# Leaving out 17 waits of a mixer step and aligning TensorE's loop in a megakernel of a recurrent mixer and experts

## The chip, the cores and the metric

The program runs on one NeuronCore of a Trainium2 chip. The metric is device time of one execution in microseconds, the median over several executions. Matmuls run on TensorE (PE), whose weight loads are shown apart (PEld); the other engines are VectorE (DVE), ScalarE (ACT), GpSimd (POOL) and SyncE (SP), which issues most DMAs. Each engine reads its own list of instructions, and engines meet only through semaphores. The granted clock of TensorE is shown as a share of full speed; it has two levels, 2.4 GHz and half of it.

## The reference

x has shape (2, 4096, 512), float32. It is normalised row by row, and the result goes two ways, whose outputs are added to x.

```
xn = layernorm(x)
x + mixer(xn) + experts(xn)
```

The mixer is a recurrence over 4096 time steps with 16 heads of 32 channels. Per head it keeps a 32x32 state:

```
sab = S @ kk
S   = S * exp(w) + outer(sab, b) + outer(v, k)
y   = S @ r
```

Here r, w, k, v, kk and b come from projections of a mix of each row with the one before it, through small two-stage (low-rank) projections, tanh and sigmoid. y is normalised per head, gets a bonus term and a gate, and is projected by `output`. The experts route the 8192 rows to 8 experts with 1024 rows each by a balanced assignment, and each runs a 512-2048-512 network with gelu.

## The kernel before

The mixer (`time_mix`) cuts time into tiles of 64 steps for both sequences, 128 rows in all. There are 64 tiles. Inside a tile the recurrence is solved in two chunks of 32 steps with matrices of 32x32: the inverse of a triangular matrix is built by doubling, in the five stages `inverse_stage(k)` for k = 1, 2, 4, 8 and 16 (line 1028, 64 small matmuls each), and scores between queries and keys are made by `score("u", m)` and `score("y", m)` for m = 0 to 5 (line 1043).

The work is a software pipeline with five parts: N (norm of the rows), A (projections), B (scores), C (inverse, state), D (normalise, gate, output). One call of `step` issues one part of each for five different tiles. `step` is called for five steps of filling, then in a hardware loop (`nc.Fori`) whose body has LONG = 28 steps written out and which runs twice, then for seven steps at the end. Behind the mixer come the experts, with the routing between their matmuls.

The order on each engine is the order of the calls in `on_tensor`, `on_vector` and so on; nothing reorders it. In a step TensorE goes, among other things, through the stages k = 1, 2, 4, 8, 16 of the inverse, `low("low_k", 2)` (line 1004) between k=8 and k=16, `key_of` (line 995), `low_second` (line 1189) and the scores, one after another.

With its 45 wait instructions a step has 3345 instructions on TensorE: 1650 weight loads and 1650 matmuls beside them.

Of the kernel before, what the change touches and what calls it, by code (L numbers as in the profile page):

```python
# [9 lines left out]
B, T, C = 2, 4096, 512  # L10
# [7 lines left out]
ROW = C + 4  # L18
SETS = 4
LONG = 28  # L20

class Steps:
# [96 lines left out]
def time_mix(nc, core, dram):  # L120

    pe, dve, act, pool = core.pe, core.dve, core.act, core.pool
    with ExitStack() as ctx:
# [862 lines left out]
        def on_tensor(e, turn, on, out, got):  # L987
            at = COLUMNS[turn % 2]
            Ns, A, Bs, Cs, D = (n in on for n in "NABCD")
# [18 lines left out]
            def inverse_stage(k, half):  # L1008

                if half == 0:  # L1010
                    clear(e, f"S{k}")
                    clear(e, f"S{k}+")
                    if k == 1:
                        if "C.rows1" in dve.was:
                            e.wait_ge(dve.old, dve.ago("C.rows1"))
                        e.wait_ge(pool.old, pool.ago("B.e1"))
                    else:
                        e.wait_ge(act.sem, act[f"C.S{k // 2}"])
                        e.wait_ge(pool.sem, pool[f"C.b{k // 2}"])
                taken = {1: slice(0, N), 16: slice(N, 2 * N)}.get(k, slice(0, 2 * N))  # L1020
                by = raw_of(0) if k == 1 else grow
                for i in range(half * HALF_U // 2, (half + 1) * HALF_U // 2):
                    for n in (i, i + HALF_U):
                        turned_in = TURN * (n // HALF_U) * (k in (4, 16))
                        turned_out = TURN * (n // HALF_U) * (k in (2, 8))
                        for h in range(HG):
                            rows, to = head((h + turned_in) % HG), head((h + turned_out) % HG)
                            mm = e.matmul(both_banks[to, n * 2 * N + taken.start:n * 2 * N + taken.stop], by[rows, blk(n)],  # L1028
                                          got["ew"][rows, n * 2 * N + taken.start:n * 2 * N + taken.stop],
                                          start=True, stop=True, skip_group_check=True)  # L1030
                if half:
                    mm.then_inc(pe.sem, pe.step(f"C.S{k}"))

            def score(q, *which):

                for m in which:
                    clear(e, f"{q}{m}")
                    e.wait_ge(dve.sem, dve["B.kk0"])
                    e.wait_ge(pool.sem, pool[f"B.q{q}"])
                    n0, n1 = UNITS[m]  # L1040
                    for n in range(n0, n1):
                        for h in range(HG):
                            mm = e.matmul(BANK[f"{q}{m}"][head(h), (n - n0) * 2 * KEYS:(n - n0 + 1) * 2 * KEYS],  # L1043
                                          queries[q][head(h), blk(n)], keys[head(h), n * 2 * KEYS:(n + 1) * 2 * KEYS],
                                          start=True, stop=True, skip_group_check=True)
                    mm.then_inc(pe.sem, pe.step(f"B.{q}{m}"))
# [134 lines left out]
                mm.then_inc(pe.sem, pe.step("A.decay"))  # L1181

            def low_second():
                for name in ("mk", "aaa", "ma"):
                    clear(e, name)
                e.wait_ge(act.sem, act["A.k"])
                for g in range(G):
                    for i, name in enumerate(("key", "mk", "aaa", "ma")):
                        mm = e.matmul(BANK[name][:, g * P:(g + 1) * P], wt["low_w2"][head(i), g * P:(g + 1) * P], hid4[head(i), :],
# [139 lines left out]
        step(-1, 3, "NABC")  # L1329
        step(0, 4, "NABCD")  # L1330
        turns = (tiles - 8) // LONG
        with nc.Fori(0, turns) as part_of_tiles:
            for i in range(LONG):
                step(part_of_tiles * LONG + (i + 1), SETS + 1 + i, "NABCD")
# [575 lines left out]
```

## Time and profile before

| | us |
|---|---|
| median of 3 runs | 5907.34 |
| lowest, highest | 5901.49, 5909.01 |
| the profiled execution | 5900.49 |
| its span, first to last instruction | 5898.6 |
| TensorE busy | 5437.2 (92%) |
| VectorE busy | 3741.3 (63%) |
| ScalarE busy | 2014.6 (34%) |

The mean granted clock is 0.972. The mixer fills the span up to about 3950 us, its loop runs from 232.6 to 3619.8 us; the experts fill the rest. Busy shares add up instructions, and small matmuls on different quarters of the array overlap, so busy TensorE is not TensorE at its peak. Idle time in front of a group of instructions is put down to what ended it. "issue" means that nothing in the profile ended it.

### The profile page before, as it was taken

Reading aid. Unit: us, or ns where it says so; the run is one execution under the profiler, and the core shown is the slowest. Engines: PE = TensorE matmul, PEld = TensorE weight load, DVE = VectorE, ACT = ScalarE, POOL = GpSimd, SP = SyncE. Lnnn points to the kernel's source line nnn. Section 1 sums busy time; section 2 is a strip of 40 time slices with the busy share of each in tenths; the row PEclk is TensorE's granted clock in tenths of the full one; section 3 lists DMA queues with packets and bytes.
Section 4 is the critical chain, followed back from the end, with each engine's and each line's share of the span. In section 5 each row is a group of like instructions: output and inputs, shape, how many; then the busy total and the mean of one; then the engine's idle time right before and its main releaser. Section 6 shows DMA issues by size and latency. Waiting matters only on the chain. (4 is left out here: it accounts for less than half of the span.)

```text
span 5898.6 us, 243936 instructions
## 1 busy us (share of the span) xinstructions
PE 5437.2 (92%) x110664; PEld 3805.1 (65%) x110664; DVE 3741.3 (63%) x9004; ACT 2014.6 (34%) x3659; POOL 1396.8 (24%) x1156
## 2 busy tenths in 40 slices
PE   6999999999989999899999999975999999999998
PEld 6777777777777777777777777752444444444443
DVE  6788888788888788878888888845232232232310
ACT  4444444444444444444444444420000000000000
POOL 1222222222222222222222222212022022121220
PEclk9999999999999999999999999987999999999999
DMA  1001000010100000010000000003112112112110
GB/s 62 23 18 25 18 21 22 18 25 18 25 18 23 21 20 24 18 25 18 23 20 23 21 20 23 16 16 97 61 50 93 50 52 102 50 52 99 39 64 14
DMA packets 108638, 211.07 MB, mean 36 GB/s; under 512 B 25553, under 2 KB 26705, under 8 KB 107089
## 3 DMA queue, kind: packets, MB, share of 16 engines
q1 hardware_dynamic: 92240, 144.91, 8.4%
q0 software_dynamic: 15360, 50.48, 2.6%
q8 instruction: 878, 14.39, 1.0%
q14 instruction: 160, 1.30, 0.1%
HBM read 144.60 MB, written 50.72 MB: 33 GB/s over the span
## 5 line engine op out<-in xcount | busy, mean ns | idle before, releaser
L392 DVE COPY_PREDICATED time_raw<-time_known,w_bank 128x96 f32<-128x96 int32 (+6 forms) x3072 | 816.7, 274 | 214.0 <-PE w_bank L1043 128.5
L1862 PE MATMUL moe_bank<-moe_w,moe_hidden 128*128 128x512 f32 x2048 | 930.4, 597 | 0.0
L1849 PE MATMUL moe_bank<-moe_hT,moe_w 128*128 128x512 f32 x2048 | 924.3, 594 | 1.5 <-DVE moe_hT L1743 1.5
L1764 ACT ACTIVATE moe_hidden<-moe_bank,moe_b 128x512 f32<-128x512 f32 x256 | 175.9, 687 | 1635.3 <-PE moe_bank L1849 1635.3
L1849 PEld LDWEIGHTS moe_bank<-moe_hT,moe_w 128*128 128x128 f32 x2048 | 386.5, 190 | 471.7 <-issue 469.8
L1862 PEld LDWEIGHTS moe_bank<-moe_w,moe_hidden 128*128 128x128 f32 x2048 | 379.8, 190 | 429.7 <-issue 428.2
L909 POOL TENSOR_TENSOR time_grow<-time_eye,time_grow 128x512 f32<-128x512 f32 x256 | 371.7, 1452 | 1131.6 <-DVE time_grow L418 1131.6
L1028 PE MATMUL w_bank<-time_ew,time_grow 32*32 32x64 f32 x32768 | 403.8, 218 | 160.4 <-issue 143.6
L1028 PEld LDWEIGHTS w_bank<-time_ew,time_grow 32*32 32x32 f32 x32768 | 350.7, 104 | 199.4 <-issue 157.2
L1043 PE MATMUL w_bank<-time_keys,time_queries_u 32*32 32x160 f32 x8192 | 362.5, 309 | 31.5 <-issue 20.3
L1743 DVE COPY moe_hT<-moe_bank 128x512 f32<-128x512 f32 x64 | 44.2, 691 | 501.0 <-PE moe_bank L1834 501.0
L661 ACT COPY time_ew<-w_bank 128x1024 f32<-128x1024 f32 x192 | 193.9, 1010 | 467.4 <-DVE time_grow L418 467.1
L1043 PE MATMUL w_bank<-time_keys,time_queries_y 32*32 32x160 f32 x8192 | 330.9, 297 | 17.4 <-DVE time_mixed L507 15.6
L1043 PEld LDWEIGHTS w_bank<-time_keys,time_queries_y 32*32 32x32 f32 x8192 | 234.5, 105 | 111.2 <-DVE time_k L527 35.6
L1043 PEld LDWEIGHTS w_bank<-time_keys,time_queries_u 32*32 32x32 f32 x8192 | 241.3, 109 | 97.3 <-issue 30.9
L995 PE MATMUL w_bank<-time_xf,time_key_w 128*128 128x128 f32 x2048 | 284.6, 296 | 11.8 <-issue 11.8
L405 DVE SCALAR_TENSOR_TENSOR time_lerp<-w_bank,time_maa,time_xx 128x128 f32<-128x128 f32 x1024 | 283.7, 339 | 13.9 <-PE w_bank L1097 12.0
L995 PEld LDWEIGHTS w_bank<-time_xf,time_key_w 128*128 128x128 f32 x2048 | 264.9, 209 | 31.1 <-issue 31.0
L995 PE MATMUL w_bank<-time_xf,time_receptance 128*128 128x128 f32 x2048 | 282.7, 287 | 0.3 <-issue 0.3
L1802 POOL DMA_INDIRECT out<-moe_result,moe_slots x64 | 69.3, 1083 | 876.1 <-DVE moe_result L1753 861.8
L995 PEld LDWEIGHTS w_bank<-time_xf,time_value 128*128 128x128 f32 x2048 | 255.7, 196 | 31.6 <-issue 31.3
L418 DVE STREAM_TRANSPOSE time_grow<-w_bank 128x512 f32<-128x512 f32 x256 | 182.7, 714 | 139.8 <-PE w_bank L1028 139.6
(226 smaller groups left out, 9421.5 us busy)
## 6 DMA issues: line engine op xcount, KB each, us to landing
moe_w<-in_w SPq DMA_DIRECT2D x64, 1024.0 KB, 7.4
mid_xn<-time_xn_rows SPq DMA_DIRECT2D x128, 129.0 KB, 2.5
time_x_rows<-in_x SPq DMA_DIRECT2D x128, 128.0 KB, 2.7
time_base<-in_x SPq DMA_DIRECT2D x128, 128.0 KB, 3.0
mid_acc<-time_mixed SPq DMA_DIRECT2D x128, 128.0 KB, 2.4
mid_scores<-time_rated SPq DMA_DIRECT2D x128, 2.0 KB, 1.7
moe_b<-in_b SPq DMA_DIRECT2D x8, 256.0 KB, 12.8
time_key_w<-in_w_key_w SPq DMA_DIRECT2D x1, 1024.0 KB, 5.3
```

The lines of the kernel that those rows point to most:

```text
L392: e.copy_predicated(by_raw[:, "uy".index(q), n0:n1, :, 0:8 * j + 8], known[:, "uy".index(q), :, :, mine].to_broadcast([P, n1 - n0, 2, 8 * ...
L405: e.scalar_tensor_tensor(grp(lerp, g), grp(BANK[f"delta{f}"], g), wt["maa"][:, f * G + g:f * G + g + 1], grp(xx, g), ALU.add, ALU.mult).th ...
L418: e.transpose(chunks(grow), rest_of(both_banks)).then_inc(dve.sem, dve.step(f"C.t{k}"))
L661: e.copy(col(got["ew"]), inv_bank).then_inc(act.sem, act.step(f"C.S{k}"))
L909: e.tensor_tensor(chunks(grow), every_unit(wt["eye2"]), chunks(grow), ALU.subtract).then_inc(pool.sem, pool.step(f"C.b{k}"))
L995: mm = e.matmul(ps[:, o * P:(o + 1) * P], weight[:, g * width + o * P:g * width + (o + 1) * P], rhs_of(g), start=g == 0 and (o == 0 or not ...
L1028: mm = e.matmul(both_banks[to, n * 2 * N + taken.start:n * 2 * N + taken.stop], by[rows, blk(n)], got["ew"][rows, n * 2 * N + taken.start: ...
L1043: mm = e.matmul(BANK[f"{q}{m}"][head(h), (n - n0) * 2 * KEYS:(n - n0 + 1) * 2 * KEYS], queries[q][head(h), blk(n)], keys[head(h), n * 2 * ...
L1764: e.activation(hidden[now % 4][:, :], up[now % 3][:, :], ACT.Gelu_apprx_tanh, bias=b1[:, x * FC + k:x * FC + k + 1]).then_inc(act.sem, act ...
L1802: e.indirect_dma_start(dram["out"], slot(x, t), tile(result, t), None).then_inc(core.stored, 16)
L1849: got = e.matmul(up[now % 3][:, :], w1[:, g * F + k * P:g * F + (k + 1) * P], hT[x % 2][:, g * CAP + half * HALF:g * CAP + (half + 1) * HA ...
L1862: got = e.matmul(down[t][:, :], hidden[now % 4][:, t * P:(t + 1) * P], tile(w2, k), start=k == 0, stop=k == FC - 1)
```

## The change

The order on every engine stays. Three places lose waits on TensorE:

- `inverse_stage` no longer waits for the former readers of its two banks, except at k=1, and not for C.rows1 of the step before;
- `score` waits for the keys (B.kk0) and the queries (B.qu, B.qy) only in its first unit, m = 0;
- `low_second` has one wait, on A.tail, for its four.

That makes 28 wait instructions in a step for 45, and 3328 instructions for 3345. Lines behind line 18 move by one or two in the new file.
```diff
+PAGE = 256
@@ inverse_stage
                 if half == 0:
-                    clear(e, f"S{k}")
-                    clear(e, f"S{k}+")
                     if k == 1:
-                        if "C.rows1" in dve.was:
-                            e.wait_ge(dve.old, dve.ago("C.rows1"))
+                        clear(e, "S1")
+                        clear(e, "S1+")
                         e.wait_ge(pool.old, pool.ago("B.e1"))
                     else:
                         e.wait_ge(act.sem, act[f"C.S{k // 2}"])
@@ score
                     clear(e, f"{q}{m}")
-                    e.wait_ge(dve.sem, dve["B.kk0"])
-                    e.wait_ge(pool.sem, pool[f"B.q{q}"])
+                    if m == 0:
+                        e.wait_ge(dve.sem, dve["B.kk0"])
+                        e.wait_ge(pool.sem, pool[f"B.q{q}"])
@@ low_second
-                for name in ("mk", "aaa", "ma"):
-                    clear(e, name)
-                e.wait_ge(act.sem, act["A.k"])
+                e.wait_ge(act.sem, act["A.tail"])
@@ time_mix
         turns = (tiles - 8) // LONG
+        nc.tensor.addr_align(PAGE, offset=154)
         with nc.Fori(0, turns) as part_of_tiles:
```

On TensorE, from the second score unit to the third in a step of the loop, the kernel before has this. In brackets stand the engines whose semaphores the instruction, and the wait instructions ahead of it, wait for; w_bank is PSUM, time_ew and time_grow the two factors of the inverse, time_xf the mixed rows.

```order
L1043 MATMUL w_bank<-time_keys,time_queries_u 32x160 [waits pool_steps0,dve_steps0]
L1043 MATMUL w_bank<-time_keys,time_queries_u 32x160 x11
L1028 MATMUL w_bank<-time_ew,time_grow 32x64 [waits act_steps0,pool_steps0]
L1028 MATMUL w_bank<-time_ew,time_grow 32x64 x63
L1004 MATMUL w_bank<-time_xf,time_low_k 128x128 [waits dve_steps0]
L1004 MATMUL w_bank<-time_xf,time_low_k 128x128 x3
L995 MATMUL w_bank<-time_xf,time_key_w 128x128 [waits act_steps0]
L995 MATMUL w_bank<-time_xf,time_key_w 128x128 x7
L1028 MATMUL w_bank<-time_ew,time_grow 32x32 [waits act_steps0,pool_steps0]
L1028 MATMUL w_bank<-time_ew,time_grow 32x32 x63
L1043 MATMUL w_bank<-time_keys,time_queries_u 32x160 [waits pool_steps0,dve_steps0]
L1043 MATMUL w_bank<-time_keys,time_queries_u 32x160 x11
```

The same stretch of TensorE after the change:

```order
L1043 MATMUL w_bank<-time_keys,time_queries_u 32x160 [waits dve_steps0]
L1043 MATMUL w_bank<-time_keys,time_queries_u 32x160 x11
L1027 MATMUL w_bank<-time_ew,time_grow 32x64 [waits pool_steps0,act_steps0]
L1027 MATMUL w_bank<-time_ew,time_grow 32x64 x63
L1005 MATMUL w_bank<-time_xf,time_low_k 128x128 [waits dve_steps0]
L1005 MATMUL w_bank<-time_xf,time_low_k 128x128 x3
L996 MATMUL w_bank<-time_xf,time_key_w 128x128 [waits act_steps0]
L996 MATMUL w_bank<-time_xf,time_key_w 128x128 x7
L1027 MATMUL w_bank<-time_ew,time_grow 32x32 [waits pool_steps0,act_steps0]
L1027 MATMUL w_bank<-time_ew,time_grow 32x32 x63
L1043 MATMUL w_bank<-time_keys,time_queries_u 32x160 [waits dve_steps0]
L1043 MATMUL w_bank<-time_keys,time_queries_u 32x160 x11
```

No matmul has moved. The score units have lost POOL's semaphore; the two stages of the inverse have one wait instruction in front of them for two, and still wait for ACT and POOL.

## Rows read from the trace of the kernel before

**Rows 1.** The page, parts 1 and 3: busy us; queue, packets, MB, share of 16 engines.
```profile
PE 5437.2 (92%) x110664; PEld 3805.1 (65%) x110664; DVE 3741.3 (63%) x9004; ACT 2014.6 (34%) x3659; POOL 1396.8 (24%) x1156
...
q8 instruction: 878, 14.39, 1.0%
```
**Rows 2.** Waits of PE: who waited for whom: us in total, times, longest us.
```profile
PE w_bank L1028 <- issue: 158.6, 110, 2.8
...
PE w_bank L1189 <- ACT time_tail L755: 15.3, 62, 1.4
```
**Rows 3.** Timeline of PE, stage k=2, loop steps one and two: start, us, group, idle before.
```profile
242.93 1.07 PE L1028 MATMUL w_bank<-time_ew,time_grow 32*32 32x64 f32 x85
245.89 0.68 PE L1028 MATMUL w_bank<-time_ew,time_grow 32*32 32x64 f32 x43 [1.89 <-issue]
...
304.07 1.00 PE L1028 MATMUL w_bank<-time_ew,time_grow 32*32 32x64 f32 x76
```
**Rows 4.** DMA from 254.8 to 256.0 us (packets, MB, share); timeline of low_k.
```profile
q8 instruction: 1, 0.02, 5.9%
...
257.28 1.37 PE L1004 MATMUL w_bank<-time_xf,time_low_k 128*128 128x128 f32 x8 [2.04 <-DVE time_grow L418]
```
**Rows 5.** Windows, the loop body's two turns: us; busy of each engine; clock; DMA.
```profile
232.60:1927.40 1694.80, 1558.86 (x46200) 1282.96 (x46200) 1400.51 (x3503) 797.88 (x1486) 453.24 (x366) 0.98 0.09 21
1927.40:3619.80 1692.40, 1561.09 (x46201) 1285.27 (x46201) 1394.33 (x3498) 796.25 (x1482) 447.66 (x362) 0.98 0.09 21
```
**Rows 6.** Windows of single steps: us; PE, PEld, DVE, ACT, POOL busy; clock; DMA.
```profile
232.60:293.70 61.10, 56.32 (x1650) 46.57 (x1650) 49.76 (x125) 28.65 (x53) 16.22 (x13) 0.97 0.09 21
1142.50:1204.50 62.00, 57.20 (x1651) 47.90 (x1651) 49.86 (x126) 28.64 (x53) 16.25 (x13) 0.94 0.08 21
2836.50:2897.20 60.70, 55.96 (x1651) 46.48 (x1651) 49.78 (x126) 28.65 (x53) 16.24 (x13) 0.97 0.09 21
3741.10:3801.20 60.10, 54.77 (x1650) 44.95 (x1650) 49.89 (x125) 28.59 (x53) 16.25 (x13) 1.00 0.07 17
1441.80:1499.60 57.80, 54.63 (x1651) 44.96 (x1651) 49.95 (x126) 28.33 (x53) 16.23 (x13) 1.00 0.09 22
957.20:1019.60 62.40, 55.87 (x1650) 45.82 (x1650) 49.82 (x126) 28.54 (x53) 16.25 (x13) 0.97 0.08 21
```
**Rows 7.** Timeline of PE in the steps from 2836.5, 3741.1 and 3679.4 us.
```profile
2849.57 0.67 PE L1028 MATMUL w_bank<-time_ew,time_grow 32*32 32x64 f32 x43 [1.63 <-issue]
...
2861.26 1.05 PE L1004 MATMUL w_bank<-time_xf,time_low_k 128*128 128x128 f32 x8 [2.34 <-DVE time_raw L392]
2862.15 3.34 PE L995 MATMUL w_bank<-time_xf,time_key_w 128*128 128x128 f32 x16
...
3765.28 1.16 PE L1004 MATMUL w_bank<-time_xf,time_low_k 128*128 128x128 f32 x8 [1.79 <-DVE time_raw L392]
3766.28 1.95 PE L995 MATMUL w_bank<-time_xf,time_key_w 128*128 128x128 f32 x16
...
3770.35 0.33 PE L1028 MATMUL w_bank<-time_ew,time_grow 32*32 32x32 f32 x25 [1.12 <-issue]
...
3708.83 0.33 PE L1028 MATMUL w_bank<-time_ew,time_grow 32*32 32x32 f32 x17 [1.49 <-issue]
```
**Rows 8.** Timeline of PE in the step from 1441.8 us: its groups with over 0.2 us of idle time.
```profile
1445.81 0.32 PE L1028 MATMUL w_bank<-time_ew,time_raw 32*32 32x32 f32 x13 [0.51 <-issue]
...
1460.79 1.43 PE L1043 MATMUL w_bank<-time_keys,time_queries_u 32*32 32x160 f32 x36 [0.33 <-issue]
...
1464.66 0.66 PE L1028 MATMUL w_bank<-time_ew,time_grow 32*32 32x64 f32 x42 [1.43 <-issue]
...
1475.83 1.17 PE L1189 MATMUL w_bank<-time_hid,time_low_w 32*128 32x128 f32 x32 [0.23 <-ACT time_tail L755]
...
1490.26 0.75 PE L1043 MATMUL w_bank<-time_keys,time_queries_y 32*32 32x160 f32 x16 [0.29 <-DVE time_mixed L507]
```
**Rows 9.** Timeline of PE at the start of the loop body's second turn.
```profile
1927.44 1.09 PE L1122 MATMUL w_bank<-time_ident,time_xn_rows 128*128 128x128 f32 x4 [3.97 <-PEq L341]
```

## The prediction

> **What bounds the kernel now.** I read the shares first: TensorE (PE) is busy 5437.2 of 5898.6 us [rows 1], so the question is what its idle time is made of. The waits view then shows that in the mixer this is mostly no wait for data. 158.6 us stand before the 32x32 matmuls of line 1028 with the releaser "issue", 110 times, which means that nothing in the profile held them back; the longest regular wait on another engine, for ACT at line 1189, takes 15.3 us over 62 steps [rows 2].
>
> The timeline shows where those stops sit. In the loop's first step (from 232.6 us) TensorE runs 85 matmuls of the stage at line 1028, stands still for 1.89 us and runs the other 43. In the next step the same stage is cut after 76 [rows 3]: 9 matmuls earlier, each with its own weight load, so about 18 instructions. A step has 1650 matmuls, 1650 weight loads [rows 6] and 45 wait instructions, together 3345, and 3345 is 13 times 256 and 17 over. A grid of 256 instructions laid over TensorE's program would slide by 17 a step, as the stops do. The DMA view names the grid: queue 8 moved 878 packets of kind "instruction", 14.39 MB, 16.4 KB each [rows 1], which is 256 instructions of 64 bytes, and one of them ran in the 1.2 us in the middle of the 2.04 us stop before line 1004 [rows 4]. So a page of 256 instructions is fetched as the sequencer comes to its end, and TensorE stops if what is queued before the boundary lasts less than the fetch. Counting from the stops, every page of the kernel before starts at the same place, and the loop's first instruction stands at slot 153 of its page.
>
> I then laid the boundaries over the step. Most of the 13 cost nothing, because slow 128x128 matmuls are queued or the stage starts with a wait during which the sequencer runs ahead. They cost where the 256-instruction stages of line 1028 are half consumed. The step from 1441.8 us has three stops, 0.51, 0.33 and 1.43 us [rows 8], and takes 57.8 us; the step from 957.2 us, with its boundaries half a page further, takes 62.4 [rows 6].
>
> **The change part by part.** 17 waits go, so a step has 3328 instructions, exactly 13 pages, and every step of the loop has the boundaries at the same places. The alignment stands ahead of the loop's register move: the move gets slot 154, the loop's first wait 155, and the first boundary comes 101 instructions into each step, then every 256. I placed the 13 in the new order: ten fall where the steps before lose nothing or under 0.2 us. Three matter.
>
> First, 613 instructions in: 170 slots into the stage k=2 of line 1028, after 85 matmuls. That is the place of the first loop step: 1.89 us in one step and 1.63 in another [rows 3, 7]. I take 1.8.
>
> Second, 1381 in: one matmul into the four of low_k (line 1004). In the loop's first step the boundary stands one matmul earlier, at the head of low_k, and costs 2.04 us [rows 4]; the others read are 2.34 and 1.79 [rows 7]. One more 128-wide matmul of cover is worth 0.1 (16 of them take 1.95 us [rows 7]), so 1.9.
>
> Third, 1637 in: 105 matmuls into stage k=16. After 103 it cost nothing in the step from 2836.5 us and 1.12 us in the step from 3741.1; after 111 it cost 1.49 [rows 7]. The difference between the first two is the clock: the second stop let the granted clock fall (0.97 over the step from 2836.5, 1.00 over the one from 3741.1 [rows 6]), the 16 matmuls of line 995 then took 3.34 us and not 1.95 [rows 7], and that longer stretch covered the fetch. So each step pays one of two: 1.4 us of lower clock, or 1.1 us of a third stop. Four of the five steps that have this place paid the clock. I take 1.4, and 0.3 for a second stretch at the lower clock in one step out of four or five (0.94 over the step from 1142.5 [rows 6]).
>
> The base is the step from 1441.8: 57.8 less 0.51, 0.33 and 1.43 is 55.5 [rows 6, 8]. New step: 55.5 + 1.8 + 1.9 + 1.4 + 0.3 = 60.9. As a control, the four steps before with their boundaries there took 61.1, 62.0, 60.7 and 60.1, mean 61.0 [rows 6]. The step before is, on average over its phases, (1694.8 + 1692.4)/56 = 60.5 with the two ends of the loop body in it [rows 5]; TensorE stands 3.97 us at such an end [rows 9], I take 5 us with what follows, so 60.3 without. Both kernels have the two ends. The difference is +0.5 to +0.7; with 0.1 off for the later place of the second boundary, +0.55 a step. The 56 loop steps and the four full steps behind them (two instructions further, same places) make 60: +33 us.
>
> The removed waits themselves. They are passed already when they are reached, as far as their engines tell: later waits of the same engine cover them. What they cost is bounded by idle time. In the step from 1441.8 TensorE is idle 57.8 - 54.63 = 3.17 us, of which 2.27 are the three stops and 0.23 + 0.29 are waits on ACT and DVE that the change keeps [rows 6, 8]. 0.38 us is left for all the rest. So removing 17 gives between nothing and 0.38 us a step; at the very most 0.9, if the idle time before lines 1189 and 1043 (a reader of two of the removed and one) went with them. I take 0.05, nearer to nothing, since almost all idle time of that step has another name: -3 us.
>
> The alignment pads once, before the loop, with idle instructions: from nothing to 255 of them. No row shows one; the trace's cheapest bounds are 0 and the spacing of a small matmul in its stage, 1.07 us for 85 [rows 3], 13 ns each, 3 us for 255. I take 0 to 1. Steps ahead of the loop and the experts behind it keep their work; their pages shift, but the waits view names no "issue" before the experts' matmuls of 512 columns.
>
> Sum: 5900.5 (the profiled execution; its span is 5898.6) + 33 - 3 = 5930. The median of the runs shown is 5907.3, the range 5901.5 to 5909.0, so the profiled execution lies 7 us under it, and part of that may come on top. I keep 5930, +0.4% on the median.
>
> The Trainium skill, "Runtime: NRT & Kernel Launch", section "Instruction fetch mechanics", says that the sequencer fetches the next 256-instruction page while it executes the current one, and that a crossing is "mostly hidden". By that rule all phases cost alike and the change would be worth only its waits, 5907 or a little less. The trace agrees on the page of 256 and on ten of the 13 crossings, and not on the others: the stops of 1.4 to 2.3 us move with the grid [rows 3, 7]. This is the second rival below, reckoned from rows.
>
> **The rivals.**
> The third stop and the lower clock both. For it: a stop of 1.49 us stands only 6 matmuls on [rows 7], and the waits that go change how far the sequencer is ahead. Against it: in the four steps at a lower clock line 995 covered the fetch. It adds 1.1 us in four of five steps, +53: 5983. It decides if the fetch at instruction 1637 starts more than 0.5 us later than now.
> The places don't matter as much as I read: the stops and the stretches of lower clock average out, the removed waits give back 0.2 to 0.4 us a step, and nothing moves beyond 0.2%: 5907. For it: four control steps are few, with a spread of 1.9 us.
> Faster: the wait instructions are on the path. Some stand before the very instructions that show idle time, lines 1189 and 1043, and a sequencer that has 17 fewer to handle is further ahead at each boundary. If it gives the full 0.9 us a step, -54, and the second stop shrinks by a third, -0.6 a step, -36, the sum is 5900 + 33 - 90 = 5843. It decides once the waits return over 0.6 us a step. Against it: the step from 1441.8 has no more than 0.38 us of idle time that isn't named after a page or another engine [rows 6, 8].
> The alignment doesn't land there. If it were without effect, the loop would begin 49 slots earlier, at 106, with the first boundary after 150: the steps like it took 62.4 us or more [rows 6], +2.1 a step, 6026. If it counts from another origin, any phase is possible, down to 57.8, -2.5 a step: 5750.
>
> **How the numbers follow.** Forecast 0.45, third stop with lower clock 0.10, no change 0.22, faster by the waits 0.15, misplaced 0.08, half of it to each side. A difference under 0.2%, 12 us, can't be told from none. The forecast itself spreads by the clock (0.3 us a step either way, 18 us) and lies above 5919 in about 8 of 10. Slower: 0.37 + 0.10 + 0.04 + 0.04 = 0.55; same 0.25; faster 0.20. The forecast's own range is 5912 to 5950. The range of 8 in 10 takes in no change, half of the fast rival and most of the third stop: 5880 to 5970.
>
> **What would show it.** In the profile after: every loop step's stage k=2 splits 85 and 43 with 1.6 to 1.9 us of "issue" between; low_k splits 1 and 7 with 1.7 to 2.3 us; stage k=16 splits at 105 in steps at full clock, and only there; no stop in stages k=1, 4 and 8 inside the loop, where now they wander. "issue" on line 1028 is then some 110 us, with more before low_k. Steps differ by the clock alone, near 60.8 us. It would be wrong if the splits stand elsewhere (misplaced), if the two stops are under 1.3 us (the waits held the sequencer back), or if a step without any stop is shorter than 55.5 us (the waits were on the path).

## The result, and the profile after

| | median us | lowest to highest | runs | ratio to before (95%) |
|---|---|---|---|---|
| before | 5905.6 | 5901.5 to 5909.9 | 6 | |
| after | 5933.8 | 5924.0 to 5941.0 | 6 | 1.0047 (1.0034 to 1.0059) |

The changed kernel is slower by 0.47%, 28 us. Its profiled execution is the slowest of its six (5941.0 us, span 5939.2), so the difference of the two traces, 40.6 us, is larger than that of the medians.

The page of the kernel after, parts 1 and 3: TensorE's work has not grown, and a few fewer pages of instructions are fetched [rows 1].

```profile
PE 5428.0 (91%) x110664; PEld 3811.6 (64%) x110664; DVE 3733.7 (63%) x9004; ACT 2023.2 (34%) x3659; POOL 1405.7 (24%) x1156
...
q8 instruction: 874, 14.32, 1.0%
```

Its waits of TensorE (total us, times, longest). Against [rows 2] "issue" before the stages of short matmuls (now line 1027) has grown from 158.6 to 182.7 us, and a second entry, 98.3 us at low_k (line 1005), was not among the large ones before. The wait for ACT has shrunk from 15.3 to 12.8 us.

```profile
PE w_bank L1027 <- issue: 182.7, 114, 2.4
PE w_bank L1005 <- issue: 98.3, 56, 2.1
...
PE w_bank L1187 <- ACT time_tail L756: 12.8, 64, 1.4
```

The timeline of the loop step that starts at 425.6 us, its groups around the stops (start, us, group, idle time before). These answer to [rows 3, 4, 7].

```profile
435.94 1.06 PE L1027 MATMUL w_bank<-time_ew,time_grow 32*32 32x64 f32 x85
439.08 0.67 PE L1027 MATMUL w_bank<-time_ew,time_grow 32*32 32x64 f32 x43 [2.08 <-issue]
...
448.36 0.38 PE L1005 MATMUL w_bank<-time_xf,time_low_k 128*128 128x128 f32 x1
450.42 0.94 PE L1005 MATMUL w_bank<-time_xf,time_low_k 128*128 128x128 f32 x7 [1.69 <-issue]
451.20 1.95 PE L996 MATMUL w_bank<-time_xf,time_key_w 128*128 128x128 f32 x16
453.08 1.09 PE L1027 MATMUL w_bank<-time_ew,time_grow 32*32 32x32 f32 x105
455.31 0.30 PE L1027 MATMUL w_bank<-time_ew,time_grow 32*32 32x32 f32 x20 [1.15 <-issue]
```

The stage k=2 is cut after 85 of 128 matmuls, low_k after 1 of 8, the stage k=16 after 105. All 56 loop steps have the first two cuts, and 42 of 56 the third; k=1, k=4 and k=8 are never cut inside the loop. Idle time, as I counted it over the timeline of all 56: k=2 mean 1.75 us (1.51 to 2.08), low_k mean 1.76 (1.34 to 2.10), k=16 mean 1.34 where it occurs (0.84 to 2.08).

Each of these stops goes with a fetched page. The DMA view from 447.8 to 449.0 us, around the start of the stop at low_k (448.73 to 450.42 us), has one packet:

```profile
q8 instruction: 1, 0.02, 5.8%
```

It starts at 447.9 us, 0.8 us before TensorE stops, and TensorE goes on 1.4 us after it has ended. So it is with all 154 stops of the loop, read from the trace's packet times: the last packet of queue 8 starts 0.1 to 1.7 us before TensorE stops, and TensorE goes on 1.2 to 1.6 us after that packet's end.

The next step back, from 363.4 us, shows the other course. The clock row under it is a windows row of 390.90 to 394.10 us (us; busy of PE, PEld, DVE, ACT, POOL; granted clock; DMA).

```profile
390.06 1.05 PE L1005 MATMUL w_bank<-time_xf,time_low_k 128*128 128x128 f32 x7 [2.07 <-issue]
390.90 3.51 PE L996 MATMUL w_bank<-time_xf,time_key_w 128*128 128x128 f32 x16
```
```profile
390.90:394.10 3.20, 3.20 (x16) 3.20 (x16) 2.83 (x7) 0.63 (x2) 1.29 (x2) 0.50 0.02 5
```

Directly after the second stop the granted clock is 0.50, the lower level of 1.2 GHz. The 16 matmuls of line 996 take 3.51 us and not 1.95, and stage k=16 is not cut. In the step from 970.5 us the stretch of lower clock begins earlier, 14.1 us into the step and behind the first stop; line 996 then runs at full clock and k=16 is cut:

```profile
997.41 1.95 PE L996 MATMUL w_bank<-time_xf,time_key_w 128*128 128x128 f32 x16
...
1002.13 0.30 PE L1027 MATMUL w_bank<-time_ew,time_grow 32*32 32x32 f32 x20 [1.75 <-issue]
```

Single steps and whole parts, after (same columns), to be read against [rows 5, 6]:

```profile
425.60:485.60 60.00, 54.31 (x1651) 44.71 (x1651) 49.76 (x126) 28.58 (x53) 16.24 (x13) 1.00 0.09 21
363.40:425.60 62.20, 57.32 (x1650) 47.75 (x1650) 49.78 (x126) 28.67 (x53) 16.24 (x13) 0.95 0.08 21
970.50:1032.40 61.90, 55.92 (x1650) 46.31 (x1650) 49.83 (x126) 28.56 (x53) 16.25 (x13) 0.97 0.09 21
...
237.90:3650.20 3412.30, 3113.18 (x92401) 2572.78 (x92401) 2785.56 (x6998) 1601.82 (x2966) 906.11 (x726) 0.98 0.09 21
3650.20:3834.80 184.60, 167.11 (x4950) 138.75 (x4950) 149.41 (x376) 85.76 (x159) 48.74 (x39) 0.97 0.08 19
```

The same two stretches of before:

```profile
232.60:3619.80 3387.20, 3119.94 (x92401) 2568.23 (x92401) 2794.84 (x7001) 1594.13 (x2968) 900.89 (x728) 0.98 0.09 21
3619.80:3801.20 181.40, 165.52 (x4950) 136.06 (x4950) 149.50 (x375) 85.67 (x159) 48.71 (x39) 0.99 0.08 20
```

So of the 40.6 us between the two spans, 5.3 lie ahead of the loop (237.9 less 232.6), 25.1 in it (60.93 us a step in place of 60.49), 3.2 in the three full steps behind it and 7.0 in what follows (2104.4 in place of 2097.4). The loop's two totals have chance in them: the one step that passes from the body's first turn to its second took 68.5 us before and 63.0 after, by its stretches of lower clock. The 54 steps that are neither the first nor this one last 60.33 us before and 60.85 after. Of the first, 3.65 us are one gap at the loop's entry, which before did not have:

```profile
237.92 1.09 PE L1122 MATMUL w_bank<-time_ident,time_xn_rows 128*128 128x128 f32 x4 [3.65 <-SPq L307]
```

### The profile page after: what moved, and what is told of

Same layout as the page of the kernel before. It is cut to its first block and busy times, and to the rows that moved or that the text cites. A ratio compares the mean times of both kernels' runs of the same rounds, so it can differ in the third digit from the quotient of the medians.

```text
span 5939.2 us, 242899 instructions
## 1 busy us (share of the span) xinstructions
PE 5428.0 (91%) x110664; PEld 3811.6 (64%) x110664; DVE 3733.7 (63%) x9004; ACT 2023.2 (34%) x3659; POOL 1405.7 (24%) x1156
## 5 line engine op out<-in xcount | busy, mean ns | idle before, releaser
L1043 PE MATMUL w_bank<-time_keys,time_queries_u 32*32 32x160 f32 x8192 | 349.4, 302 | 9.7 <-issue 2.2
L946 POOL TENSOR_TENSOR time_ew<-time_eye,time_ew 128x512 f32<-128x512 f32 x64 | 87.9, 1374 | 756.6 <-DVE time_ew L490 756.6
## 6 DMA issues: line engine op xcount, KB each, us to landing
moe_b<-in_b SPq DMA_DIRECT2D x8, 256.0 KB
```

Source lines behind the costliest of these rows:

```text
L946: e.tensor_tensor(rest_of(out["ew"]), every_unit(wt["eye2"]), sum_of(out["ew"]), ALU.subtract).then_inc(pool.sem, pool.step("B.e1"))
```

## The experiments

The theory, A: a step's time is set by which matmuls stand at the page boundaries, and the alignment put them at a poor place. The rivals: the removed waits matter by themselves; aligning costs by itself; the clock falls for other reasons. "Slot" is the slot of 256 at which the loop's first instruction stands; the step column is the loop's time in one traced execution over 56, with both ends of the body in it. Two executions with the same stops can differ in it by 0.7 us, as after and "155, padding at start" do, so it is no measure of small differences.

| run | slot | median us | ratio to before (95%) | us a step |
|---|---|---|---|---|
| before | 153, slides by 17 | | | 60.49 |
| after | 155 | 5933.8 | 1.0047 (1.0034 to 1.0059) | 60.93 |
| waits only | 106 | 6084.3 | 1.0290 (1.0264 to 1.0316) | 63.37 |
| slot 238 | 238 | 5752.5 | 0.9725 (0.9701 to 0.9749) | 57.85 |
| waits as filler | 155, slides | 5983.1 | 1.0110 (1.0090 to 1.0131) | 61.58 |
| alignment only | 155, slides | 5922.5 | 1.0004 (0.9991 to 1.0018) | 60.64 |
| slot 196 | 196 | 5842.7 | 0.9869 (0.9853 to 0.9886) | 59.37 |
| slot 0 | 0 | 5757.7 | 0.9730 (0.9716 to 0.9744) | 57.78 |
| 238, padding at start | 238 | 5736.2 | 0.9697 (0.9682 to 0.9712) | 57.88 |
| waits spread | 155, slides | 5927.1 | 1.0025 (1.0011 to 1.0038) | 60.83 |
| 248, padding at start | 248 | 5729.2 | 0.9697 (0.9678 to 0.9717) | 57.89 |
| 155, padding at start | 155 | 5914.7 | 1.0018 (1.0005 to 1.0032) | 60.25 |
| stop inside k=16 | 155, slides | 6011.7 | 1.0178 (1.0158 to 1.0198) | 62.37 |

Each ratio is to runs of before on the same chip, and for small differences it is the ratio that counts; their medians there were 5915.9, 5916.8 and 5905.0 us for the three groups of runs in the order of the table.

### The waits alone

```
-        nc.tensor.addr_align(PAGE, offset=154)
```

> The 17 waits are left out as in the changed kernel, the alignment is not made, so the loop's first instruction lies at slot 106 and each of its steps still crosses the same 13 places. Theory A (the time is set by which matmuls lie at the crossings): the crossings move by 49 instructions, to after 150 instructions of a step and every 256 from there; steps of before with their first crossing there lasted 62.4 to 63.0 us, so about 62.9 a step, +2.6 x 60 over before's 60.3: about 6060 us, 6020 to 6075. Theory B (the changed kernel is slower through its alignment's padding or through the lost waits, the places do not matter): with the padding gone 5900 to 5935 us.

Measured 6084.3 us, 9 above the range of A; B is out. The steps run from 61.5 to 65.1 us, and the one over the body's end takes 69.0. One of them, from 551.2 us, and its cuts at the new places:

```profile
551.20:616.00 64.80, 59.20 (x1651) 48.74 (x1651) 49.86 (x126) 28.55 (x53) 16.22 (x13) 0.92 0.08 20
```
```profile
564.53 0.41 PE L1027 MATMUL w_bank<-time_ew,time_grow 32*32 32x64 f32 x19 [1.67 <-issue]
570.75 0.69 PE L1027 MATMUL w_bank<-time_ew,time_grow 32*32 32x64 f32 x44 [0.31 <-issue]
...
583.12 1.82 PE L1043 MATMUL w_bank<-time_keys,time_queries_u 32*32 32x160 f32 x23 [2.11 <-issue]
584.87 3.78 PE L996 MATMUL w_bank<-time_xf,time_key_w 128*128 128x128 f32 x16
```

Leaving the waits out is therefore the half of the change that fixes the boundaries' places, and without the alignment it fixes them at a place that costs 2.9 us a step more than before. The alignment of the changed kernel takes back 2.4 of these.

### Slot 238

```
-        nc.tensor.addr_align(PAGE, offset=154)
+        nc.tensor.addr_align(PAGE, offset=237)
```

> The changed kernel with the loop's first instruction at slot 238 of 256 in place of 155. Theory A (places): the crossings come after 18 instructions of a step and every 256 from there; steps of before with a first crossing near there lasted 58.2 to 58.5 us, so about 2 us a step less than before's 60.3 and 2.5 less than the changed kernel's 60.9: 5906 + 4 (entry) - 1.9 x 60 = about 5795 us, 5770 to 5820. Theory B (alignment or lost waits cost, the places do not): 5930 to 5950 us, more by the longer padding (132 in place of 49).

Measured 5752.5 us, below A's range and far from B. The stops of the step from 365.3 us, all of its groups with idle time before them:

```profile
369.44 0.32 PE L1027 MATMUL w_bank<-time_ew,time_raw 32*32 32x32 f32 x13 [0.61 <-issue]
380.03 1.16 PE L1172 MATMUL w_bank<-time_rk,time_bonus_ones 128*128 128x128 f32 x8 [0.16 <-DVE time_mixed L454]
384.46 1.42 PE L1043 MATMUL w_bank<-time_keys,time_queries_u 32*32 32x160 f32 x36 [0.25 <-issue]
387.99 0.64 PE L1027 MATMUL w_bank<-time_ew,time_grow 32*32 32x64 f32 x40 [1.09 <-issue]
398.97 1.17 PE L1187 MATMUL w_bank<-time_hid,time_low_w 32*128 32x128 f32 x32 [0.18 <-ACT time_tail L756]
413.39 0.75 PE L1043 MATMUL w_bank<-time_keys,time_queries_y 32*32 32x160 f32 x16 [0.28 <-DVE time_mixed L508]
```
```profile
365.30:422.70 57.40, 54.60 (x1650) 44.88 (x1650) 50.09 (x126) 28.34 (x53) 15.71 (x13) 1.00 0.09 22
```

The step is the twin of before's step from 1441.8 us [rows 6, 8], stop for stop. The whole loop has only 8 stretches at 0.50, against 38 before and 44 after. The clock is a part of what made the forecast too high: before's four steps with a boundary at this place (from 533.9, 1441.8, 2228.3 and 3136.1 us) took 58.2, 57.8, 59.3 and 57.6 us, mean 58.2, and one of these four has such a stretch, where the loop at slot 238 has one in seven steps. Shorter stops, 2.0 us a step and not 2.2, are as large a part, and the rest is that I took 58.4.

The gap at the loop's entry is larger here:

```profile
246.27 1.09 PE L1122 MATMUL w_bank<-time_ident,time_xn_rows 128*128 128x128 f32 x4 [9.64 <-PEq L342]
```

### The 17 waits back, in one row

```
             on_tensor(nc.tensor, turn, on, out, got)
+            if on == "NABCD":
+                for _ in range(35):
+                    nc.tensor.wait_ge(act.sem, act["A.tail"])
```

(The compiler puts two waits into one instruction and lets a last one ride on the next matmul: 35 make 17 instructions.)

> The changed kernel with 17 instructions put back at the end of each full step, as waits on a semaphore that has been reached since long: a step has 3345 instructions again and its crossings slide by 17 from step to step as in before, but the 17 waits are gone from the stages where they stood. Theory A (the waits cost nothing where they stood, the sliding places give the mean): as before plus the entry's padding, 5905 + 4 = about 5909 us, 5900 to 5918, steps 60.2 to 60.4. Rival (the removed waits cost 0.38 to 0.9 us a step on TensorE and the alignment takes it back and more): 5850 to 5885 us.

Neither: 5983.1 us. The filler was no neutral filler. From the trace, the step from 420.08 us and the one behind it:

```profile
420.08 0.63 PE L1122 MATMUL w_bank<-time_ident,time_xn_rows 128*128 128x128 f32 x4 [1.70 <-PEq L342]
...
478.14 0.63 PE L1122 MATMUL w_bank<-time_ident,time_xn_rows 128*128 128x128 f32 x4 [1.79 <-PEq L342]
```

17 waits that are all reached stop TensorE for 1.7 us or more when they stand in a row, which is at least 0.1 us each; how much more the queue hides there, the trace doesn't show. The run says nothing on what the removed waits had cost where they stood, since the new stop also gives the fetches and the other engines time. It had to be made again with the waits apart.

### The alignment alone

```
 (before, with all its waits)
+        nc.tensor.addr_align(256, offset=154)
```

> The kernel before with the alignment alone; its steps keep 3345 instructions, so the loop's first lies at slot 155 in the first turn only and the crossings go on sliding. Theory A: no difference but the padding's own price at the loop's entry, at most the 3.7 us seen there in the changed kernel: 5906 to 5912 us. Rival (the alignment itself is what costs, through its padding or what stands behind the loop): 5925 to 5940 us.

Measured a ratio of 1.0004 (0.9991 to 1.0018), 5922.5 beside 5915.9 us: no difference; its loop took 60.64 us a step beside 60.49. The directive moves the loop by two slots here and pads almost nothing. In a loop whose step is no multiple of 256 it has nothing to hold.

### Slots 196 and 0

```
-        nc.tensor.addr_align(PAGE, offset=154)
+        nc.tensor.addr_align(PAGE, offset=195)      (and offset=255)
```

> The changed kernel with the loop's first instruction at slot 196; the crossings come after 60 instructions of a step and every 256 from there: 316, 572, 828, 1084, 1340 and 1596 lie near or in the stages of short matmuls. Theory A (the places set the time): steps of before with a first crossing near 60 lasted 59.2 to 59.4 us, between those of slot 238 (58.4 by the same rows) and of slot 155 (60.7); the run of slot 238 gave 57.7, so 58.6 to 59.4 a step here: 5830 us, 5795 to 5860, with 90 slots of padding at the entry (6.6 us). Theory C (any place other than those of slot 155 is equally good, since only the matmuls at 613 and 1381 matter): 5752 less the shorter padding, 5745 to 5755.

> The changed kernel with the loop's first instruction at slot 0: crossings at 0, 256, 512, 768, 1024, 1280 and 1536. By the durations of before's sliding steps (57.96 against 58.4 us at 18) it should be 0.4 us a step faster than slot 238: 5730 us. By the stops of single crossings (1024: 1.1 us and 1280: 0.8 to 1.1 in the run with the sliding steps, against 0.3 at 1042 and 1.2 at 1298 at slot 238) it should be 0.4 a step slower: 5780 us. Theory A holds in either case; it tells which of the two rows is to be used for a forecast.

5842.7 and 5757.7 us. At slot 196 the steps are cut after 64 of k=2 and after 109 of k=8, as the step from 481 us shows, and take 59.4 us:

```profile
493.77 0.84 PE L1027 MATMUL w_bank<-time_ew,time_grow 32*32 32x64 f32 x64 [1.27 <-issue]
504.31 0.41 PE L1027 MATMUL w_bank<-time_ew,time_grow 32*32 32x64 f32 x19 [1.19 <-issue]
```

Theory C is out: places other than 155 are not equally good. Slot 0 came out between its two estimates, 57.78 against 57.85 us a step at slot 238, with somewhat longer stops and fewer stretches of lower clock (4 in the loop). Both kernels paid for their padding at the entry:

```profile
242.56 1.09 PE L1122 MATMUL w_bank<-time_ident,time_xn_rows 128*128 128x128 f32 x4 [6.60 <-PEq L342]
```
```profile
246.72 1.08 PE L1122 MATMUL w_bank<-time_ident,time_xn_rows 128*128 128x128 f32 x4 [10.97 <-PEq L342]
```

3.65, 6.60, 9.64 and 10.97 us for 49, 90, 132 and 150 slots: 73 to 75 ns a slot each time. With no padding, in the run with the waits alone, there is no such gap.

### The padding moved to the program's start

```
+        nc.tensor.addr_align(PAGE, offset=197)
         nc.tensor.wait_ge(core.consts_in, CONSTS)
 ...
-        nc.tensor.addr_align(PAGE, offset=154)
```

> Slot 238 as in the fastest run so far, with the 132 slots of padding moved from the loop's entry to the program's first instructions, where TensorE waits 16.3 us for the constants; the steps of the start and of the end get the same places. If the padding costs some 73 ns a slot on TensorE wherever it is executed in front of work: 9.6 us less at the entry, nothing at the start, and 3 to 8 us less in the two full or nearly full steps before the loop: 5752 - 10 - 5 = 5737 us, 5730 to 5745. If the gap at the entry is not the padding but the loop's own entry: 5745 to 5755.

Measured 5736.2 us. The loop starts at 225.3 and not at 246.2 us: 9.6 us of padding and 11 us in the steps ahead of the loop, where 3 to 8 were expected and whose boundaries have moved too. The first matmul waits for the constants as before, the padding lies inside that wait:

```profile
16.55 1.84 PE L255 MATMUL w_bank<-time_cent,time_lerp 128*128 128x8 f32 x8 [16.55 <-DVE time_gcent L247]
```

### The 17 waits back, one by one

```
+            def spare():
+                if on == "NABCD":
+                    e.wait_ge(act.sem, act["A.tail"])
+                    e.wait_ge(act.sem, act["A.tail"])
 ...
             if A:
                 low_second()
+            spare()                (and behind 16 more stages)
```

> As the run with 17 waits in one row at the end of a step (steps of 61.5 us, each with a new stop of 1.7 us at its first matmul), but the 17 are spread one by one over the last third of the step, behind 17 different stages. Crossings slide again by 17 a step. If a single wait that is long reached is hidden by the queue and only many in a row run it dry: the stop at the step's first matmul goes and steps last 61.5 - 1.7 = 59.8 (should the 17 removed waits have cost some 0.5 us a step where they stood) or 60.3 (should they have cost nothing): 5880 or 5910 us. If each wait costs its 0.1 us wherever it stands: steps 61.4, 5975 us.

Measured 5927.1 us, ratio 1.0025 (1.0011 to 1.0038). The stop at the step's first matmul is gone: what costs there is the row. But some single waits showed; this step from 534.2 us has new idle times at lines 1114 and 1056:

```profile
576.72 1.95 PE L1114 MATMUL w_bank<-time_output,time_mixed 128*128 128x512 f32 x4 [0.19 <-DVE time_raw L393]
...
582.47 0.75 PE L1043 MATMUL w_bank<-time_keys,time_queries_y 32*32 32x160 f32 x16 [0.18 <-DVE time_mixed L508]
583.52 1.52 PE L1056 MATMUL w_bank<-time_by_values,time_vT 32*32 32x96 f32 x64 [0.30 <-ACT time_yT L672]
```

Over all 56 steps line 1114 waits 34 times, 6.8 us in all, and line 1056 56 times, 15.3 us, while the usual wait at line 1043 has fallen from before's 14.3 us to 10.3. That is 0.32 us a step that the filler itself costs: 60.83 - 0.32 = 60.51, beside before's 60.49. So close an agreement is partly luck, since single executions differ by more. By the medians (10.3 us over before, of which 2.3 are this kernel's gap at the loop's entry and 18 the filler) the removed waits come out at some 10 us, about 0.2 us a step. So where they stood, the 17 waits cost nothing that shows clearly, and hardly more than 0.2 us a step.

### The best place, and the changed kernel's own with its padding at the start

```
-        nc.tensor.addr_align(PAGE, offset=197)
+        nc.tensor.addr_align(PAGE, offset=207)      (and offset=114)
```

> Padding at the program's start as in the fastest run, the loop's first instruction at slot 248: crossings after 8 instructions of a step and every 256 from there (264, 1032, 1288). At 0 the steps lasted 57.70 us and at 18 57.67 to 57.75. If the time changes smoothly with the place: 57.5 to 57.9 a step, 5736 us, 5722 to 5748. If two crossings that lie just behind a stage's start (1032 in the first score stage, 264 in the first inverse stage) trade against each other sharply: more than 0.5 us a step off, above 5765 or below 5706 us.

> The changed kernel's own slot (155), with its 49 slots of padding at the program's start. If the changed kernel is slower by the places of the crossings: its steps stay at 60.9 us, only the entry's 3.6 us and some 2 to 5 us in the two steps before the loop go: 5934 - 4 - 3 = 5927 us, 5920 to 5932, still above the kernel before. If a good part of its loss lies in aligning inside the program: 5905 us or less.

Slot 248 gave 5729.2 us: on the plateau from 238 over 248 to 0, not to be told apart from slot 238, and with it the fastest kernel of the study, 3% below before.

Slot 155 with the padding at the start gave 5914.7 us, 12 runs from 5892 to 5939, ratio 1.0018 (1.0005 to 1.0032). That is under my range by 5 us and above the 5905 of the other case, and the loss that is left is at the bound of what can be told from none. Its trace is of its fastest run: stops as in the changed kernel (98.8 us at low_k, 57 times), 26 stretches of lower clock in the loop in place of 44, 60.25 us a step. Ahead of the loop 8.1 us went (3.65 of padding, the rest steps with better places). Between this run and the changed kernel's profile, the loop differs by 38 us with the stops at the same places; 6 us are shorter stops (247 us in all in place of 253), and the rest goes with the 18 fewer stretches of lower clock. That much of a single run of this kernel is chance. The medians are another matter: the ratio fell by 0.29%, 17 us, of which 8 lie ahead of the loop. Where the other 9 went is open.

### A stop put among the short matmuls

```
                 inverse_stage(16, 0)
+                if on == "NABCD":
+                    for _ in range(35):
+                        e.wait_ge(act.sem, act["C.S8"])
                 inverse_stage(16, 1)
```

> As the run with 17 filler instructions in one row at the end of each step (a stop of 1.7 us in front of the step's first matmul, steps of 61.5 us, 34 windows of the lower clock in the loop), but the row stands in the middle of the stage k=16, among the short matmuls, behind a semaphore that this stage has waited for already. Theory C1 (the clock falls after a stop among the short matmuls, not after one at the step's first): far more than 34 windows, 55 to 110, each some 1.4 to 2.1 us: steps of 62.0 to 63.5 us, 6015 to 6100 us. Theory C2 (where the stop stands does not matter to the clock): 30 to 40 windows, steps near 61.5, 5970 to 5995 us.

Measured 6011.7 us, by the ratios 0.7% or 40 us more than with the same row at the step's end, and 59 stretches of lower clock in the loop where that run had 34. 31 of them begin 30 to 35 us into a step, directly behind the new stop; there that run had 10. C1 holds, at the low end of the count that it gave and 3 us under its time. One place of each kind was tried, so it isn't shown if it is the short matmuls around the stop that matter or something else of the place.

The two kernels' first loop steps are alike up to low_k, and so the pair shows one more thing. With the row at the step's end:

```profile
252.40 0.67 PE L1027 MATMUL w_bank<-time_ew,time_grow 32*32 32x64 f32 x43 [1.51 <-issue]
263.69 0.94 PE L1005 MATMUL w_bank<-time_xf,time_low_k 128*128 128x128 f32 x7 [1.63 <-issue]
268.59 0.30 PE L1027 MATMUL w_bank<-time_ew,time_grow 32*32 32x32 f32 x20 [1.16 <-issue]
```

With the row inside k=16:

```profile
253.44 0.67 PE L1027 MATMUL w_bank<-time_ew,time_grow 32*32 32x64 f32 x43 [1.51 <-issue]
...
264.73 0.94 PE L1005 MATMUL w_bank<-time_xf,time_low_k 128*128 128x128 f32 x7 [1.63 <-issue]
267.38 0.75 PE L1027 MATMUL w_bank<-time_ew,time_grow 32*32 32x32 f32 x64
269.74 0.71 PE L1027 MATMUL w_bank<-time_ew,time_grow 32*32 32x32 f32 x62 [1.60 <-issue]
```

The second half of k=16 runs through. The row moves the boundary from 105 to 96 matmuls into the stage, but there is no cut there either. What differs is the pause 32 matmuls ahead of it, which gave the fetch its time; that this is the cause is argued from the pair and not tried alone. A stretch of lower clock ahead of the boundary did the same in the changed kernel's step from 363.4 us.

## Why the prediction was right

**The places.** The three stops stand where the count put them, at 85, 1 and 105 matmuls, the first two in every loop step, the third in 42 of 56, and no page stop stands elsewhere. This was the core of the argument, and five fixed slots confirm it: by sliding steps of before with the same boundaries I expected 62.9, 58.4, 59.3, 60.9 and 58.0 us for slots 106, 238, 196, 155 and 0, and the loops gave 63.4, 57.9, 59.4, 60.9 and 57.8. The order is right in all of them and the size within 0.6 us. One proof of the fetch was misread: the packet shown in [rows 4] runs from 254.8 us on, and the stop from 255.24 to 257.28 us, so it lies at the stop's start and not in its middle. As in the changed kernel, TensorE goes on 1.4 us after the packet's end; the stop is longer than what is left of the fetch.

**The two stops.** 1.8 and 1.9 were taken, 1.75 and 1.76 measured. That one matmul further into low_k saves anything isn't shown: in the three full steps behind the loop the boundary stands at the head of low_k again, and the stop is 1.85, 1.51 and 1.94 us, mean 1.77.

**The third place: right sum, wrong mechanism in part.** "Pays one of two" was too tidy. Over the 59 full steps from the loop's first on I counted 20 steps with the third stop at full clock, 8 without it and one stretch of lower clock, 6 without it and two stretches, and 25 with both. What decides is where the stretch lies. All 14 steps of the loop without the third stop have a stretch of lower clock that begins between 24.6 and 27.5 us into the step, around the second stop and over line 996, and no other step of the loop has one there. The same holds without exception for the 9 such steps of the run with slot 155 and the padding at the start. So "pays one of two" is right for a stretch at that place. What the forecast missed is that stretches begin elsewhere too, and that many steps have none.

In its outcome, though not by its condition (a later fetch), the rival of both together is true in more than four steps of ten. It did not bring its +53 us, since the stretches of lower clock come less often than in the four steps read: 20 steps have none. Clock and third stop together cost a step about 60.9 less 55.1 less 3.5, 2.3 us, where I had 1.7. That is also why "issue" on the short matmuls is 182.7 us and not the 110 I named: the third stop was no exception. 23 of the 44 stretches in the loop begin 10 to 15 us into a step, about the first stop.

**The base.** 55.5 came from one step of before. The clean step from 425.6 us leaves 60.0 - 2.08 - 1.69 - 1.15 = 55.1; at slot 238 the step from 365.3 us leaves 57.4 - 0.61 - 0.25 - 1.09 = 55.45, the old base again. I had named a step under 55.5 us without its stops as a sign that the waits were on the path, and 55.1 is under it. At slot 238, where the same waits are gone, the sign doesn't come, so at most the place and the waits together could bring it. Of the 0.4 between the two kernels 0.3 is busy time of TensorE (54.60 against 54.31), and 0.16 is the idle time before line 1172 that only the second of the two has. Steps of before at the changed kernel's places give no clear answer. The step from 3741.1 us, at full clock, leaves 55.6 without its stops, beside 55.1; the one from 2836.5, with one stretch of lower clock, 56.7 beside 56.3 to 56.8; the one from 1142.5, with two, 58.0 beside 58.1 (the changed kernel's steps with as many stretches and no third stop). What these tenths are stays open.

The mean of 60.9 came out right because 0.4 too much here and 0.2 too much for the two stops stand against 0.6 too little for the third place. That they cancel is luck.

**The removed waits.** -3 us is not contradicted, but not measured either. At slot 238 the sum that gave 0.38 us of unexplained idle time gives 57.4 - 54.60 - 1.95 - 0.18 - 0.28 = 0.39, so this time is still there and was not that of the waits; without its stops the step is 0.1 us shorter than its twin (55.45 against 55.55). The spread filler puts the waits between nothing and 0.2 us a step. The rival with the waits on the path, 5843 us, is out by the run with the waits alone. What it assumed does exist, a wait instruction takes some time of the sequencer, but it showed only in a row and, one by one, at two places of 17.

**The alignment.** Its padding is the term that was mis-sized: 0 to 1 us taken, 3 us given as the most for 255 slots, 3.65 us measured for 49. The nearest row, the spacing of a small matmul, was the wrong neighbour by a factor of almost six.

**Ahead of the loop and behind it.** I took these to stay; they did not quite. 1.6 us ahead beside the padding, and 7.0 us in what follows the full steps, were added in the traces. The part behind the full steps took 2104.4 and 2104.7 us in the two kernels of slot 155, 2093.6 and 2093.4 in the two of slot 238, and 2107.2 in the run with the waits alone, so it, too, goes by the place; which of its stages pays was not tried. The forecast also counted four full steps behind the loop; there are three, and the fourth stands ahead of it.

**The sum.** From profiled execution to profiled execution the forecast was 33 - 3 = 30 us, and 40.6 came: 28.3 in the loop and the full steps behind it, and 12.3 in the padding, the start and the end, which were taken at nothing or 1 us. That the median of 5933.8 lies within 4 us of 5930 is partly luck, since before's profiled execution lies 5 us under its median and after's 7 over. The 28.3 itself, from one execution each, can be off by tens of us. What the experiments do show beyond chance is the order of the places.

**"No difference" and the skill.** The Trainium skill ("Runtime: NRT & Kernel Launch", "Instruction fetch mechanics") calls a crossing "mostly hidden". Ten of 13 crossings a step are, in the steps shown at slots 155 and 238. The others and what follows from them are worth some 6% between the best and the worst slot that were run (ratios 0.9697 and 1.0290, 5729 and 6084 us). In the step shown at slot 238 the two dearest take 0.61 and 1.09 us. The second rival falls, but not by far: with its padding at the start the changed kernel is slower by 0.2% only.

## What to carry to other kernels

When a loop's body is a multiple of the fetched page, its boundaries stand still, and then the place is a choice to be measured: here the slot of one instruction moves the same program from 2.9% slower to 3.0% faster. Look in the timeline for stops named "issue" inside long runs of short matmuls, count the instructions between them, and try to put the boundaries where slow instructions or a wait stand ahead. A stop at the head of a stage can carry an engine's name and still be the page's, as that at low_k before [rows 4]: look there for a packet of kind "instruction". Put the padding where the engine waits anyway.

## What the runs showed that I had not expected

- A padding slot costs TensorE's sequencer 73 to 75 ns, over 49 to 150 slots.
- Seventeen waits that are long reached, in a row, stopped TensorE for 1.7 to 2.2 us at the step's first matmul, the loop's entry and its turn aside, and for 1.60 to 1.79 us inside k=16, about 0.1 us each; single ones showed as 0.2 to 0.3 us in two places of a step and not at all in the others.
- TensorE goes on 1.2 to 1.6 us after the packet with the page has ended, at all 154 stops in the loop after.
- Stops of 1.5 us and more among short matmuls are often followed by stretches at the granted clock of 0.50: with the row inside k=16, one begins within 6 us of the end of the row's stop in 37 of 56 steps, and with the row ahead of a step's first matmul in 3 of 56. Fewer stops went with fewer stretches, though not in proportion: idle times over 1 us in the loop's steps and stretches were 155 and 85 with the waits alone, 146 and 44 after, 103 and 38 before, 111 and 22 at slot 196, 51 and 8 at slot 238, 46 and 4 at slot 0. So a good place mostly pays twice. Which steps get such a stretch at equal stops stays open: 26 or 44 of them came with the same stops in two executions.
